# Twelve layers on one core: normalisation and router logits in phases of their own ahead of the experts, and expert results over four banks

## What is computed

```python
def _moe(x, gate, w1, w2, w3):
    xf = x.reshape(-1, D)
    probs = softmax(xf @ gate)
    w, idx = top_k(probs, TOP_K)
    comb = einsum('nk,nke->ne', w / w.sum(-1), one_hot(idx, N_EXPERTS))
    for e in range(N_EXPERTS):
        h = silu(xf @ w1[e]) * (xf @ w3[e])
        out = out + comb[:, e:e + 1] * (h @ w2[e])
x = x + _attention(_rmsnorm(x, g1), wq, wk, wv, wo)
x = x + _moe(_rmsnorm(x, g2), gate, w1, w2, w3)
```

## Time and profile before

| | us |
|---|---|
| median of the runs | 2603.59 |
| runs | 2605.23, 2603.59, 2597.24 |
| the profiled execution | 2607.98 |
| its span | 2606.2 |
| TensorE's matmuls busy | 2113.5 (81%) |
| VectorE busy | 1558.3 (60%) |
| ScalarE busy | 1176.4 (45%) |
| GpSimd busy | 758.6 (29%) |

### The profile page before, as it was taken

How to read it: one execution, slowest core, us unless ns; L and a number is a source line. 1 busy time by engine, 2 the same in 40 slices (tenths; PEclk the granted TensorE clock), 3 DMA queues, 4 the chain that set the end, 5 groups by cost and what they waited for, 6 DMA issues and landing times. The chain is left out here.

```text
span 2606.2 us, 36968 instructions
## 1 busy us (share of the span) xinstructions
PE 2113.5 (81%) x12720; PEld 1272.8 (49%) x12720; DVE 1558.3 (60%) x3628; ACT 1176.4 (45%) x2304; POOL 758.6 (29%) x937
## 2 busy tenths in 40 slices
PE   7784995767848887997898888775999798677887
PEld 4572572225622224664454444472344466567555
DVE  4677337988848883554545555453557345655665
ACT  2443437654336664224667666432445322133344
POOL 0330004643331100002565556434443000153122
PEclk8796897988859998997999999885789898698899
DMA  1000000001032200002333222102220001000000
GB/s 37 37 1 6 1 1 6 1 1 53 1 111 49 45 1 1 1 1 90 80 79 82 71 79 59 50 1 67 48 51 3 1 1 68 28 1 1 1 1 17
DMA packets 38601, 80.35 MB, mean 31 GB/s; under 512 B 7344, under 2 KB 21680, under 8 KB 37392
## 3 DMA queue, kind: packets, MB, share of 16 engines
q1 hardware_dynamic: 35952, 75.00, 10.8%
q10 hardware_dynamic: 2464, 2.99, 0.4%
HBM read 51.75 MB, written 7.34 MB: 23 GB/s over the span
## 5 line engine op out<-in xcount | busy, mean ns | idle before, releaser
L731 ACT ACTIVATE spt<-P 128x1024 f32<-128x1024 f32 (+3 forms) x256 | 221.0, 863 | 195.3 <-PE P L585 195.3
L698 DVE TENSOR_REDUCE smf<-P 128x2 f32<-128x1024 f32 (+3 forms) x256 | 254.5, 1019 | 53.6 <-PE P L574 30.7
L2274 PEld LDWEIGHTS P<-W,e_h 128*128 128x128 f32 (+1 forms) x1952 | 219.6, 190 | 61.2 <-issue 52.3
L2274 PE MATMUL P<-W,e_h 128*128 128x128 f32 (+1 forms) x1952 | 226.2, 277 | 13.3 <-DVE X L2467 13.3
L2260 PE MATMUL P<-XT,W 128*128 128x512 f32 x424 | 223.6, 625 | 12.0 <-ACT e_g L2346 8.8
L1085 POOL TENSOR_TENSOR d_e<-d_e,d_rc 128x512 f32<-128x512 f32 (+3 forms) x256 | 180.0, 725 | 177.6 <-DVE d_rc L991 147.6
L2467 DVE SCALAR_TENSOR_TENSOR X<-P,WE,X 128x128 f32<-128x128 f32 x448 | 126.1, 344 | 147.6 <-PE P L2274 147.6
L1034 ACT ACTIVATE d_e<-d_e,d_mn 128x512 f32<-128x512 f32 (+3 forms) x256 | 141.7, 554 | 130.6 <-DVE d_mn L983 130.3
L2346 ACT ACTIVATE e_g<-P 128x512 f32<-128x512 f32 x148 | 88.1, 597 | 242.0 <-PE P L2260 238.2
L2365 DVE TENSOR_TENSOR e_h<-e_g,P 128x512 f32<-128x512 f32 x148 | 101.3, 685 | 111.2 <-PE P L2264 109.9
L2264 PE MATMUL P<-XT,W 128*128 128x512 f32 x296 | 155.8, 608 | 0.9 <-DVE e_h L2365 0.9
(11 more groups left out here) (407 smaller groups left out, 4197.2 us busy)
## 6 DMA issues: line engine op xcount, KB each, us to landing
d_bt<-in_alibi SPq DMA_DIRECT2D x32, 512.0 KB, 3.7
d_moved<-d_raw SPq DMA_DIRECT2D x256, 64.0 KB, 2.4
ska<-parts_k SPq DMA_DIRECT2D x72, 64.0 KB
sqa<-parts_q SPq DMA_DIRECT2D x72, 64.0 KB
W<-in_w_L_xattn SPq DMA_DIRECT2D x1, 4291.0 KB, 13.7
W<-in_w_L_ffn SPq DMA_DIRECT2D x1, 3333.0 KB, 11.0
W<-in_w_L_ffn SPq DMA_DIRECT2D x1, 3155.0 KB, 10.1
parts_k<-sparts SPq DMA_DIRECT2D x8, 384.0 KB, 2.5
```

The lines of the kernel that those rows point to most:

```text
L698: v.tensor_reduce(MF[:, n % 2, u, :], P[:, bank:bank + 2, 0:wide(u)], AX.X, ALU.max, negate=True).then_inc(s("max"), 1)
L731: a.activation(PT[:, n % 3, :, t, N - late(t):N], P[:, BANK_T:BANK_T + 2, 0:late(t)], ACT.Exp, scale=SC).then_inc(s("exp"), 1)
L2274: last = pe.matmul(P[:, PY + j % 2, 128 * t:128 * (t + 1)], HT[rows, q % RING, blk, 128 * t:128 * (t + 1)], w2, start=n == 0, stop=n == le ...
```

## The change

Three edits.

- The norm ahead of the experts leaves `experts`. In L0, L1 and L2 a call of `normalise` on `k.Hs` stands before it, and for L3 the call stands at the end of L3's cross-attention. The copies of the steps inside `experts` go.
- `normalise` takes `logits=(stage, width)`: then TensorE, behind all four chunks' transposes, waits for each chunk's copy and runs the router's matmuls into bank 6. In `experts` the routing starts without a wait, and so does `up`.
- `down` goes round banks 4 to 7 and waits for result j-4. As bank 6 holds the logits, result 2 waits until the routing has read them.

```diff
-def normalise(k, i, src, dst, eps, rms=False, scale=None, shift=None, store=False, again=None):
+def normalise(k, i, src, dst, eps, rms=False, scale=None, shift=None, store=False, again=None, logits=None):
...
                 last.then_inc(s("turned"), 1)
+            if logits is None:
+                return
+            stage, width = logits
+            wr, ready = weights(k, stage)
+            ready(pe)
+            for c in QT_:
+                pe.wait_ge(s("xt_a" if c in turned_by_a else "xt_v"), c // 2 + 1)
+                for t in range(4 * c, 4 * c + 4):
+                    pe.matmul(P[:, 6, width * t:width * (t + 1)], k.XT[:, 128 * t:128 * (t + 1)], wr["router"], start=True, stop=True)
...
             def up(q):
-                if q == 0:
-                    xt_ready(pe, 0)
...
-                    if j == 2:
-                        turn(2)
-                        turn(3)
-                        logits()
...
-                    if j >= 2:
-                        taken(pe, j - 2)
+                    if j >= 4:
+                        taken(pe, j - 4)
+                    elif j == 2:
+                        pe.wait_ge(s("shifted"), 1)
...
-                            last = pe.matmul(P[:, PY + j % 2, 128 * t:128 * (t + 1)], HT[rows, q % RING, blk, 128 * t:128 * (t + 1)], w2,
+                            last = pe.matmul(P[:, PY + j % 4, 128 * t:128 * (t + 1)], HT[rows, q % RING, blk, 128 * t:128 * (t + 1)], w2,
...
-            turn(0)
-            turn(1)
-            w_ready(pe)
...
-            v.wait_ge(s("norm_v"), 8)
-            v.wait_ge(s("logits"), 1)
             routed()
...
-            if not STAGES[i].endswith("xattn"):
-                normalise(k, i, k.X, k.X, 1e-5, store=i == LAST - 1)
+            if not STAGES[i].endswith("xattn") or STAGES[i] == "L3_xattn":
+                normalise(k, i, k.X, k.X, 1e-5, store=i == LAST - 1, logits=(i + 1, 16) if STAGES[i] == "L3_xattn" else None)
...
-            experts(k, i, expert_units(k, i, 8, 2), False, ACT.Gelu_apprx_tanh, 8, "plain", AHEAD["L0"], 4,
-                    (k.Hs, nx, 1e-5, False, "n2w", "n2b"), hidden_in=k.Hs)
+            normalise(k, i, k.Hs, nx, 1e-5, scale="n2w", shift="n2b", logits=(i, 8))
+        experts(k, i, expert_units(k, i, 8, 2), False, ACT.Gelu_apprx_tanh, 8, "plain", AHEAD["L0"], 4, hidden_in=k.Hs)
```

More of the change, by code:

```diff
@@ L2183, in _, with experts @@
                 row_means(k, v, s, ST, k.X, range(QT * b, QT * (b + 1)), QT * (b + 1))
-def experts(k, i, units, gated, func, E, mode, ahead, steps, norm, hidden_in=None):
+def experts(k, i, units, gated, func, E, mode, ahead, steps, hidden_in=None):
     nc, P = k.nc, k.P
@@ L2218, in experts @@
         WE = k.WE[:, :, 0:E]
[L2219 to L2230, removed]
+        PG, PU, PY = 0, 2, 4
         @block.tensor
         def _(pe):
[L2234 to L2246, removed]
+            w_ready(pe)
             def up(q):
-                if q == 0:
-                    xt_ready(pe, 0)
                 x = k.XT[:, N * (q // U):N * (q // U + 1)]
@@ L2298, in _ @@
         def _(a):
[L2299 to L2313, removed]
-            apply(0)
-            apply(1)
-            copy(0)
-            apply(2)
-            apply(3)
-            copy(2)
             a.wait_ge(s("shifted"), 1)
@@ L2334, in scaled @@
                     dst = SUM2[:, c % 2, 128 * t:128 * (t + 1)] if q % U == 0 else SCALED[:, n % 2, 128 * t:128 * (t + 1)]
-                    last = a.activation(dst, P[:, PY + j % 2, 128 * t:128 * (t + 1)], ACT.Copy, scale=k.WE[:, 4 * c + t, units[q % U][1][1][0]:units[q % U][1][1][0] + 1])
+                    last = a.activation(dst, P[:, PY + j % 4, 128 * t:128 * (t + 1)], ACT.Copy, scale=k.WE[:, 4 * c + t, units[q % U][1][1][0]:units[q % U][1][1][0] + 1])
                 last.then_inc(s("scaled"), 1)
@@ L2415, in routed @@
             def routed():
-                lg = P[:, PL, 0:TILES * E].rearrange("p (t e) -> p t e", e=E)
+                lg = P[:, 6, 0:TILES * E].rearrange("p (t e) -> p t e", e=E)
                 if mode == "groups":
@@ L2476, in out @@
                     row_means(k, v, s, ST, k.X, range(4 * c, 4 * c + 4), 4 * (c + 1))
-            def apply(c):
-                for t in on_v:
-                    t += 4 * c
-                    if rms:
-                        v.tensor_scalar(dst[:, t, :], src[:, t, :], k.RS[:, t:t + 1], None, ALU.mult).then_inc(s("norm_v"), 1)
-                    else:
-                        v.tensor_scalar(dst[:, t, :], src[:, t, :], k.MV[:, t, 0:1], k.RS[:, t:t + 1],
-                                        ALU.subtract, ALU.mult).then_inc(s("norm_v"), 1)
-            def copy(c):
-                o, i_ = turned(v, c)
-                if scale is not None and shift is not None:
-                    v.tensor_scalar(o, i_, w[scale], w[shift], ALU.mult, ALU.add).then_inc(s("xt_v"), 1)
-                elif scale is not None:
-                    v.tensor_scalar(o, i_, w[scale], None, ALU.mult).then_inc(s("xt_v"), 1)
-                else:
-                    v.tensor_copy(o, i_).then_inc(s("xt_v"), 1)
-            if rms:
-                v.tensor_tensor(sq[:], mean, mean, ALU.mult).then_inc(s("small"), 1)
-                v.wait_ge(s("small"), 1)
-                v.scalar_tensor_tensor(inv[:], sq[:], eps, var, ALU.add, ALU.add).then_inc(s("small"), 1)
-                v.wait_ge(s("small"), 2)
-            else:
-                v.tensor_scalar(inv[:], var, eps, None, ALU.add).then_inc(s("small"), 1)
-                v.wait_ge(s("small"), 1)
-            v.reciprocal(inv[:], inv[:]).then_inc(s("inv"), 1)
-            v.wait_ge(s("root"), 1)
-            if not rms:
-                v.scalar_tensor_tensor(k.NM[:], mean, -1.0, k.RS[:], ALU.mult, ALU.mult).then_inc(s("nmr"), 1)
-            w_ready(v)
-            apply(0)
-            apply(1)
-            apply(2)
-            copy(1)
-            apply(3)
-            copy(3)
-            v.wait_ge(s("norm_v"), 8)
-            v.wait_ge(s("logits"), 1)
             routed()
@@ L2646, in run_stage @@
         with nc.sbuf_tensor("NX2", [128, TILES, D], F32) as nx:
-            experts(k, i, expert_units(k, i, 8, 2), True, ACT.Silu, 8, "shares", AHEAD["L1"], 4,
-                    (k.Hs, nx, 1e-5, True, "n2w", None), hidden_in=k.Hs)
+            normalise(k, i, k.Hs, nx, 1e-5, rms=True, scale="n2w", logits=(i, 8))
+        experts(k, i, expert_units(k, i, 8, 2), True, ACT.Silu, 8, "shares", AHEAD["L1"], 4, hidden_in=k.Hs)
     elif name == "L2_attn":
@@ L2658, in run_stage @@
         with nc.sbuf_tensor("NX4", [128, TILES, D], F32) as nx:
-            experts(k, i, expert_units(k, i, 4, 3), True, ACT.Silu, 4, "shares", AHEAD["L2"], 4,
-                    (k.Hs, nx, eps, True, "n2w", None), hidden_in=k.Hs)
+            normalise(k, i, k.Hs, nx, eps, rms=True, scale="n2w", logits=(i, 4))
+        experts(k, i, expert_units(k, i, 4, 3), True, ACT.Silu, 4, "shares", AHEAD["L2"], 4, hidden_in=k.Hs)
     elif name == "L3_attn":
```

4 lines of the change are left out of this document (2 added, 2 removed).

## The result

The changed kernel takes 2571.62 us (median of six runs, 2559.44 to 2578.87) against 2603.45 us for the kernel before (six runs, 2597.24 to 2605.23): a ratio of 0.9875, 95% interval 0.9844 to 0.9907. The direction was right, and both parts of the change brought a gain in the stages named for them, but the whole came out nearly twice as large. The profiled execution took 2575.28 us, with a span of 2573.1.

The account below looks back on a forecast made before the run. TensorE was taken to bound L3's expert stage, its gaps being waits for VectorE. Four banks -12.8 and the split -3.7 us made -16.5, from 2603.59 to 2587.1 us, range 2573 to 2595.

Parts of the forecast that it names:

- Which waits go, and what takes their place: L3's expert stage: four banks remove TensorE's 16 waits for VectorE, 13.3 us; only 0.5 us is lost at the end.
- What a wait is worth: L3's result matmuls: each wait priced at its idle time, 14 x 0.76 + 2 x 1.36 us; gain 12.8 us.
- a cycle of 5.99 us has 5.23 us of TensorE work: L3's result cycle: without its 0.76 us of idle time, it was to take 5.23 us.
- The new order of the start: Expert stages' starts: transposes, logits, border take 11.9 us against 13.35 in L1; saves 1.45 there, 1.55 L0, 1.4 L2, 0.85 L3.
- rival (a): Normalise phases: logits run at the high clock, 3.4 us less in each of four stages, 2573.5 us; chance 14%.
- The argument for the low clock: Logits in all four stages take 6.9 us at the low clock, by the stretch from 2252 and today's normalise phase's transposes.
- L3's start: From L3's first transposes to VectorE's first routing step: 12.75 us before, 11.9 forecast, saving 0.85 us.
- The border: Between normalise and expert phases: 0.32 us, plus 0.11 from the last logits matmul to VectorE, 0.43 in all.
- Rival (c): Phase border costs 1.4 instead of 0.43 us, a table load hides a little more: 4 to 5 us, 2591.5 us; chance 8%.
- The up-projections inside the stage: First two blocks' up-projections move into the expert stage: L0 +0.8 and -1.4 us, L1 +0.6, L2 +0.65.
- uncovered table load: Expert phase's start: ScalarE's 1.28 us load, no longer behind the logits, delays the exponential 0.63 us, in L3 0.82.
- Rival (d): Stages' wide up-projections stay at the low clock longer; slower by 0.3% needs 12 us more per stage, 2627 us at 20; 4%.

Follow-up runs that it names:

- the run with its own wait: Kernel after, with TensorE in L3 waiting ahead of each unit's pair of results until its own earlier results are done; 2575.8 us, ratio 0.9902.
- the split alone: Kernel after with two result banks again, each result waiting for j-2, norm and logits still in a phase of their own; 2592.15 us, ratio 0.9969.

## Why the prediction was right and wrong

**Which waits go, and what takes their place: right.** All sixteen stood in L3, all are gone, and no other engine came near the new cycle. At the end of the stage, where I gave back all but 0.3 us of the last wait because VectorE stands behind GpSimd, 0.21 came back (from the last burst's start to the stage's end, 6.88 us before and 6.67 after).

**What a wait is worth: wrong, and this is the larger part of the miss.** I took the idle time in the row (14 x 0.76 + 2 x 1.36) as the price. By the starts of the bursts, ten waits inside double bursts cost 1.33 each, two at chunk ends 1.93, three ahead of the shared expert's result 0.80, and the last one 0.21: 13.3 + 3.9 + 2.4 + 0.2 = 19.8 us, against 12.8. The step that failed is "a cycle of 5.99 us has 5.23 us of TensorE work": 5.23 was the sum of bursts each of which had started afresh, and unbroken the same work takes 4.66. The size of the excess, 0.57 us for most waits and 0.04 for the three ahead of the shared expert's result, goes with the coinciding starts told above. The weight loads' rows of the kernel before had 0.92 of the 1.33; the remaining 0.41 could be had from the trace only by comparing a burst of 16 with a longer one of the same matmuls. The Trainium skill (Perfetto Trace Analysis, Tensor Engine Instruction) says that TensorE's end times in a profile are estimated and not observed; the trace agrees, with two kernels in which waits that cost 0.7 us leave no idle time in the matmuls' rows.

**The new order of the start: right in L0, too slow in L1 and L2.** The sum was 4.57 + 6.9 + 0.43 = 11.9 us from first transposes to routing. L0 has 4.55 + 6.83 + 0.30 = 11.68, and with low logits L1 has 11.40 (in the run with its own wait). The clock is what I had at 14% as rival (a), for four stages; it came true in two, not in the others. The term that failed is the 6.9 us of logits in L1 and L2, which took 4.05 and 4.06. That both were high in the first trace is chance: other executions of the same work had one or the other low. With high logits L1 gained 4.3 us and L2 3.4; with low logits, in other executions, 1.1 and 0.2, near the forecast's 0.85 and 0.75. So 6.2 us of the miss are the clock of two stages. The argument for the low clock was sound as to the logits, which raised it in no run. It overlooked that the clock can rise in the transposes ahead of them: it took the one phase of the earlier trace rows, where it didn't, for the rule. What decides it from one execution to the next no run shows.

**L3's start: 1.7 us earlier, where 0.85 was forecast**, as its first eight transposes, the first two chunks, ran at the high clock: 3.91 us from the first transposes to the logits in place of L0's 4.55. From the routing's start to the first result it was 33.96 us and is 34.76: 0.80 us more, the forecast's 0.82 for the table load, and 0.80 us come back when the load is moved.

**The border: 0.30 us idle on TensorE**, near the 0.32 of a phase that ends with VectorE. Rival (c), with 1.4 us, is out. A drain of 1.38 us behind each table load, which the prediction also weighed, isn't there: the exponential of L1 starts at 1007.07, the load ended at 1007.05.

**The up-projections inside the stage: the size about right, the reason not.** Block 2's first weights are loaded 3.6 us after the stage's start in L0 (3.7 forecast) and its gate matmul starts 6.2 us after it in L1 (5.5), since the low clock held for about 5.5 us of it and not 4.2. The prediction had named a low clock of over 5 us there as a sign of being wrong, and 5.5 us it was in L1 and L2, 5.1 in L0. The rest of L1's stage is 0.7 us longer (0.6 forecast). The forecast's 0.63 us for the uncovered table load isn't what made it so: with the load moved and the clock as it was, L1 and L2 end no earlier. Rival (d) needed 8 us more at the low clock.

**The sum.** 16.5 forecast; 7.0 more from what a wait costs, 6.2 from the logits of L1 and L2, 0.9 from L3's start, give 30.6, which is what the four stages sum to; the medians differ by 31.8. What lies between is the rest of the program, whose clock differs from execution to execution by more than that.

## What to carry to other kernels

Where TensorE is the bound, the idle time shown ahead of a matmul isn't the price of the wait: here 0.76 us shown cost 1.33 in most places, 0.80 in some, and 0.21 at the stage's end, where another engine was just as late. The price is the distance between the starts of two bursts, less what the same matmuls take inside a longer unbroken burst. Look at the weight loads' rows for a gap in the midst of like loads; in one of the three kernels that row named the releaser as well. And the logits kept a high clock that they found for 3.6 us at most, so price it at both levels and see what stands ahead of it: here wide matmuls of no use, sized to TensorE's idle time, together with an early table load, paid for themselves; twice as many, alone, didn't.

## What was new about the hardware

- A wait that cost 0.7 us on TensorE left no idle time in its matmuls' rows, in two kernels; it was to be seen in the weight loads as gaps of 0.30 and 0.31 us, and as a fresh start that costs 0.41 us over sixteen loads.
- Where a result on rows 64 to 127 followed one on rows 0 to 63, or the other way round, three matmul instructions started within 4 to 6 ns of another one; ahead of a result on all 128 rows none did. In the kernel before a wait at such a place cost 0.57 us beyond the idle time shown, and one ahead of the result on all rows 0.04.
- 13.6 us of logits matmuls, with TensorE busy without a gap, stayed at 0.50. In L1 the logits began at 1.00 and were back at 0.50 some 3 us on, though TensorE had no pause.
- A pause of 1.30 us in L3's dense stretch was followed by 3.4 us at the low clock in the three-bank kernel, at both chunk ends. The kernel before has pauses of 1.36 and 1.37 us at the same places and stayed high; the split alone has 1.36 at both and fell behind the first and not behind the second. So the pause alone doesn't decide it; what does, no run shows.
- The same self-attention phase, with the same 2096 matmul instructions, took 256.6 us at a mean granted clock of 0.85 and 274.4 at 0.76. Nothing in the change bears on it, and what decides it is open.
